# Cross attention on one core: ScalarE copies each V tile out of the shared PSUM bank, GpSimd splits the copy

## What is computed

```python
x = x + cross_attention(layernorm(x), ctx_1024, ctx_1024)   # x: 2 x 256 x 256, ctx: 2 x 4096 x 256
q = scale * (Q @ Wq + bq)        # 16 heads of 64
k = K @ Wk + bk
v = V @ Wv + bv
a = softmax(q k^T)
out = (a v) @ Wo + bo
```

## Time and profile before

| | us |
|---|---|
| median of 3 runs | 1417.87 |
| the three runs | 1412.96, 1418.12, 1417.87 |
| time of the profiled execution | 1414.05 |
| span of the profiled execution | 1412.1 |
| loop over the 128 steps, from about / to about | 43 / 1175 |

### The profile page before, as it was taken

One profiled execution on the slowest core, in us unless ns is written; L12 is line 12 of the kernel. 1 busy time (PEld: TensorE's weight loads), 2 busy tenths in 40 slices (PEclk: granted clock), 3 DMA queues, 4 the chain that ended last, 5 costly groups with the idle time before them and its releaser, 6 DMA issues. The chain is left out here.

```text
span 1412.1 us, 24618 instructions
## 1 busy us (share of the span) xinstructions
PE 1315.2 (93%) x9284; PEld 1121.4 (79%) x9284; DVE 1006.2 (71%) x1375; ACT 870.5 (62%) x1700; POOL 657.0 (47%) x797
## 2 busy tenths in 40 slices
PE   5899999999999999999999999999999996589857
PEld 5788888888888888888888888888888885267734
DVE  3666678667866777678767876787678767299666
ACT  3667666676667666676667666766676663256511
POOL 5655755475547553565457545754574440000000
PEclk9999999999999999999999999999999999699879
DMA  4010000000000000110000000000000000300000
GB/s 127 16 45 2 16 1 9 8 16 1 9 9 31 16 24 31 38 31 9 2 23 1 8 2 23 1 9 1 9 1 1 1 9 1 101 0 1 1 0 15
DMA packets 24901, 22.95 MB, mean 16 GB/s; under 512 B 4432, under 2 KB 24528, under 8 KB 24784
## 3 DMA queue, kind: packets, MB, share of 16 engines
q1 hardware_dynamic: 24784, 21.38, 5.0%
HBM read 20.85 MB, written 0.52 MB: 15 GB/s over the span
## 5 line engine op out<-in xcount | busy, mean ns | idle before, releaser
L548 ACT ACTIVATE pT_hi<-psT 128x512 fp32r<-128x512 f32 x512 | 292.4, 601 | 237.6 <-PE psT L320 222.5
L623 DVE TENSOR_TENSOR pT_lo<-psT,pT_hi 128x512 fp32r<-128x512 f32 x512 | 330.3, 684 | 105.4 <-ACT pT_hi L548 104.9
L617 DVE TENSOR_REDUCE negm<-psS 128x1 f32<-128x1024 f32 x256 | 311.7, 1218 | 51.2 <-PE psS L310 51.2
L267 POOL TENSOR_TENSOR kT<-kraw,khi 64x512 fp32r<-64x512 f32 x252 | 324.9, 1289 | 0.0
L513 ACT ACTIVATE prob<-psS,negm 128x1024 f32<-128x1024 f32 x256 | 285.7, 1116 | 1.0 <-DVE negm L617 1.0
L320 PE MATMUL psT<-ident,prob 128*128 128x128 f32 x2048 | 268.5, 274 | 3.9 <-DVE pT_lo L623 3.9
L261 POOL CAST khi<-kraw 128x512 fp32r<-128x512 f32 x126 | 76.9, 610 | 418.0 <-ACT kraw L523 416.6
L336 PE MATMUL psO<-pT_hi,v 128*128 128x256 f32 x1024 | 268.5, 294 | 1.2 <-DVE pT_lo L623 0.4
L320 PEld LDWEIGHTS psT<-ident,prob 128*128 128x128 f32 x2048 | 233.1, 140 | 38.8 <-issue 11.1
L337 PE MATMUL psO<-pT_lo,v 128*128 128x256 f32 x1024 | 256.7, 283 | 0.0
L336 PEld LDWEIGHTS psO<-pT_hi,v 128*128 128x128 f32 x1024 | 196.2, 192 | 2.7 <-DVE pT_lo L623 2.6
(11 more groups left out here) (215 smaller groups left out, 1563.9 us busy)
## 6 DMA issues: line engine op xcount, KB each, us to landing
cst<-in_ctx_dram SPq DMA_DIRECT2D x12, 512.0 KB, 3.8
oT<-in_ctx_dram SPq DMA_DIRECT2D x4, 512.0 KB, 5.3
wraw<-in_L_xattn_Wk_dram SPq DMA_DIRECT2D x8, 256.0 KB, 2.7
wraw<-in_L_xattn_Wv_dram SPq DMA_DIRECT2D x8, 256.0 KB, 2.7
wraw<-in_L_xattn_Wq_dram SPq DMA_DIRECT2D x8, 256.0 KB, 2.7
wo<-in_L_xattn_Wo_dram SPq DMA_DIRECT2D x8, 256.0 KB, 2.8
ff_wdn<-in_L_ffn_w_down_dram SPq DMA_DIRECT2D x1, 704.0 KB, 8.2
ff_win<-in_L_ffn_w_gate_dram SPq DMA_DIRECT2D x1, 640.0 KB, 5.3
```

Of the source, the lines that this page charges most:

```text
L267: pool.tensor_tensor(kT[half, m // 2 % KRING, h, 1, :], raw[own, :], khi[own, :].bitcast(F32), ALU.subtract).then_inc(k_split, 1)
L548: act.activation(pT_hi[:, i % PRING, :], psT[:, t % 2, :], ACT.Copy).then_inc(ph_ok, 1)
L617: dve.tensor_reduce(negm[:, g % 2, h, qt, c:c + 1], psS[:, qt, :], AX.X, ALU.max, negate=True)\
L623: dve.tensor_tensor(pT_lo[:, i % PRING, :], psT[:, t % 2, :], pT_hi[:, i % PRING, :].bitcast(F32), ALU.subtract).then_inc(pl_ok, 1)
```

## The change

A new SBUF tile `vraw` (128 x 512, fp32, one buffer) and a new semaphore `vraw_ok`. For m >= 4 ACT no longer writes the high part of V, but copies the bank to `vraw` (`v_copy`); it waits for `v_lo` to have reached m, that is for tile m - 1 to be split, before it overwrites `vraw`. POOL makes both parts from `vraw` in the new `split_v`, behind `split_piece` of the same step: a copy, then a subtraction. DVE's `v_low` is gone from the loop. TensorE's waits for the bank (`bank_free`, the one ahead of `turn_ctx`, the one behind the loop) are for `vraw_ok` in place of `v_lo`; `values` still waits for `v_lo`. The wait for the ring slot (`av_ok`) goes from ACT to POOL. The four tiles ahead of the loop are made as before.

```diff
@@ tiles and semaphores
+        vraw = tile("vraw", [P, 2 * GD])
...
-        v_ps, v_hi, v_lo = sem("v_ps"), sem("v_hi"), sem("v_lo")
+        v_ps, v_hi, v_lo, vraw_ok = sem("v_ps"), sem("v_hi"), sem("v_lo"), sem("vraw_ok")
@@ gpsimd
+            def split_v(m):
+                wait(pool, vraw_ok, m + 1 - FIRST)
+                if m >= VRING:
+                    old = m - VRING
+                    wait(pool, av_ok, 4 * (old // GH * GH + GH - 1) + old % GH + 1)
+                heads = vraw[:, :].rearrange("p (k h d) -> p k h d", k=2, h=GH)
+                pool.tensor_copy(v[:, m % VRING, :, :, 0, :], heads).then_inc(v_hi, 1)
+                wait(pool, v_hi, m + 1)
+                pool.tensor_tensor(v[:, m % VRING, :, :, 1, :], heads, v[:, m % VRING, :, :, 0, :].bitcast(F32),
+                                   ALU.subtract).then_inc(v_lo, 1)
+                wait(pool, v_lo, m + 1)
...
                 split_piece(n + LEAD)
+                split_v(n + LEAD)
@@ tensor, bank_free
                 else:
-                    wait(pe, v_lo, min(n + LEAD, N))
+                    wait(pe, vraw_ok, min(n + LEAD, N) - FIRST)
@@ tensor, end of a context step
                     wait(pe, cst_in, 16 * (u // KT - FIRST + 1))
-                    wait(pe, v_lo, n + LEAD + 1)
+                    wait(pe, vraw_ok, n + LEAD + 1 - FIRST)
                     turn_ctx(u, cst, psW[:, :])
@@ tensor, behind the loop
-                    pe.wait_ge(v_lo, N)
+                    pe.wait_ge(vraw_ok, N - FIRST)
@@ scalar
             def v_high(m, src):
                 wait(act, v_ps, m + 1)
-                if m >= VRING:
-                    old = m - VRING
-                    wait(act, av_ok, 4 * (old // GH * GH + GH - 1) + old % GH + 1)
...
+            def v_copy(m, src):
+                wait(act, v_ps, m + 1)
+                wait(act, v_lo, m)
+                act.activation(vraw[:, :], src, ACT.Copy).then_inc(vraw_ok, 1)
...
                 if n + LEAD < N:
-                    v_high(n + LEAD, psW[:, :])
+                    v_copy(n + LEAD, psW[:, :])
@@ vector
                 p_low(n, 3)
-                if n + LEAD < N:
-                    v_low(n + LEAD, psW[:, :])
```

## The result

The changed kernel takes 1404.13 us (median of 5 runs, 1402.24 to 1408.14). The kernel before, with two more runs than stood ahead of the prediction, has its median at 1413.68. The ratio is **0.9933, 95% interval 0.9917 to 0.9949**: 0.7% faster. The forecast was 1408.0 us and -0.70%. One execution of experiment 3 took 4681 us, 3.3 times the others, and stands in no median or ratio here.

The account below looks back on a forecast made before the run. TensorE, busy 93% of the span, was taken as the bound. Minus 9.9 us on the profiled 1414.05 gave 1404.2 (-0.70%); the same share off the median 1417.87 gave 1408.0 us, range 1401 to 1416.5.

Parts of the forecast that it names:

- rival B: Next step's first bank use waits for `prep_low` and takes the gain: 1418 or 1414 if all, 1413 if half; 26%.
- sign of being wrong: Among the listed signs: a turn of the bank that waits for `ctxT_lo` for 0.4 us.
- DVE's relief: In the loop, 124 removed subtractions take 86 us off DVE's row; gain 0 apart from the context turn's wait.
- The term: Context turn comes 0.12 us after the last matmul of `values`, not 0.55: 23 steps x 0.43 = 9.9 us gained.
- POOL's tight place: Steps 11 to 15 of groups 0 to 6, where POOL also splits weights and Q: covers of 0.2 to 0.7 us.
- Cost 0: POOL's added work in steps 11 to 15 of groups 0 to 6 was to cost TensorE nothing.
- stay near 10 us: Sign of being right: the waits of `k_raw` for POOL keep their total, 10.4 us in 7 waits before.
- Rival C's point: POOL late in steps 12 to 15 once its pair exceeds about 2.7 us; near 1458 at 4.1; 8%.
- the chain of covers: At a 2.7 us pair, four pairs' delays less about 1 us of cover: 1.4 us per group, 10 in all.
- The rule: VectorE and GpSimd share an SBUF port under an exclusive lock; expected not to bite in the loop, otherwise POOL is held.

Follow-up runs that it names:

- experiment 3: The changed kernel's path for V only in the 100 steps without a context turn, the old path in the 24 with it; 1417.82 us, 1.0006 of the kernel before.
- experiments 2 to 4: The first: the changed kernel's path for V only in the 24 context steps, 1404.49 us, 0.9934 of the kernel before; the others are experiment 3 and experiment 4.
- Experiment 8: The changed kernel with the split of the next V weights moved from GpSimd to VectorE in step 11; 1397.35 us, 0.9885 of the kernel before.
- experiment 5: The changed kernel with GpSimd writing the high part of V twice, one more copy per split; 1414.37 us, 1.0002 of the kernel before.
- Experiments 7 and 8: The first: the changed kernel plus a VectorE subtraction with two SBUF inputs in steps 10 to 15, 1405.68 us, ratio 0.9942; the second is Experiment 8.
- experiment 4: The changed kernel with an unused VectorE maximum over a constant tile in place of each removed subtraction; 1402.90 us, 0.9914 of the kernel before.
- experiment 10: The changed kernel with the context turn waiting for the split of V again, not for ScalarE's copy; 1537.55 us, 1.0866 of the kernel before.

## Why the prediction was right

*The mechanism and its size.* Point by point: the turn follows at 0.12 us in all 24 steps; the wait is gone, and in 22 of the 23 steps no other stands in its place (rival B falls). The wait for `ctxT_lo` that the prediction gave as a sign of being wrong is in the table, but it was there before, as long and as often. DVE's relief is worth nothing (experiments 2 to 4); the gain is that of the context steps alone. The term was 23 x 0.43 = 9.9 us, and the 23 steps gave 10.0. Two small errors cancel in it. Per step it is 0.45 to 0.46, because the scores also follow the turn 0.03 us closer (0.53 after its start, 0.56 before). And one gives nothing: the step from 11 to 12 of group 3. The prediction worked out POOL's tight place with the times of group 1 alone, where step 11 has no context turn; in group 3 the shorter step brings the next `k_raw` ahead of the end of POOL's split. Experiment 8 shows that this is the cause: with the split of the weights of V off POOL that step falls from 9.13 to 8.67 us.

That the profiled executions differ by just the 9.9 us of the term (1414.05 and 1404.13) is luck: beside the 10.0 us their spans gain 1.6 at the start and 0.4 in other steps, and lose 2.3 behind step 0 of group 7. For the share 0.70% was forecast and 0.67% measured.

*Rival B had a thin margin.* It gave ACT 0.08 us between `oT` and `prep_high`. The row shows 0.06 (61.64 against 61.20 + 0.38). It held because `oT` moves with `values`, as the prediction argued.

*POOL.* The pair takes 610 and 1281 ns, 2.05 us from start to free; strided writes cost POOL nothing. The piece of step 12 begins at 296.12, 1.3 us after `kraw` is written, and `k_raw` of step 14 waits 0.18 us, where 0.2 was forecast:

```profile
294.10 0.69 ACT L537 ACTIVATE kraw<-psW,bkT 128x512 f32<-128x512 f32 x1 [1.39 <-POOL kT L268]
...
311.02 0.69 ACT L537 ACTIVATE kraw<-psW,bkT 128x512 f32<-128x512 f32 x1 [0.18 <-POOL kT L268]
```

This wait comes once in each of six groups and stays under the cover of 0.44 us, so step 14 keeps its 8.22 us. The seventh new entry of the table is the wait of 0.42 us in step 12 of group 3, and TensorE does see it (0.20 us of waiting, 0.45 of step length not gained). "Cost 0" was wrong by this one step. The sentence that the waits "stay near 10 us" was right in the total (11.7) and missed that their number would double.

*Rival C's point.* "The pair takes over about 2.7 us": experiment 5 is that pair, and its ratio is 1.0002: the chain of covers gave 10 us of cost there, and 10 were measured. At 3.4 us the same way of counting gave 28 us over the changed kernel, and 34 were measured; among what it left out is the wait of `values` in step 0 of the next group.

*The rule.* The lock was rightly given little weight for this kernel, for the reason named: VectorE's large operations in the loop have at most one SBUF input, and GpSimd's 124 new subtractions take 1262 to 1305 ns. That the two engines can hold each other up, experiments 7 and 8 show; the last section has the numbers.

*What was mis-sized.* The absolute time was placed 3.9 us too high, since it was taken from a median of three runs, two of which lay near 1418. The profiled execution's own time gave 1404.2. With five runs the median of before is 1413.68. The share was the sounder number.

## What to carry to other kernels

When a kernel is bound by one engine, ask of each helper not how busy it is but which of its instructions that engine waits for; here 24 of 124 moved tiles carried the whole gain, through the moment at which a shared PSUM bank was handed on. A raw copy to SBUF frees a bank after one instruction, and the slow work may then run beside the rest, provided that the waits move with it: with the wait left on the slow work the changed kernel is 133 us slower. Before loading another engine, walk its queue through the fullest stretch and add up the covers, in each kind of step: a step that the change itself shortens has less cover. The average load (64%, 68%, 73% here) does not tell a free split from one that costs 34 us.

## What the runs showed of the hardware

VectorE and GpSimd do hold each other up when VectorE's operation has two SBUF inputs. Experiments 7 and 8 show it: GpSimd's copy of 512 numbers takes 0.95 to 0.96 us in place of 0.61, and VectorE's subtraction 1.50 and 1.65 in place of 0.68. The later of the two, be it that copy or that subtraction, ends 0.46 to 0.56 us after the first has ended. VectorE's copy from SBUF to SBUF, with one input, does it too: beside it GpSimd's two-input operation takes 1.45 us in place of 1.29 in six groups of experiment 8, and in group 3 GpSimd's copy 0.87 in place of 0.61. That copy takes VectorE 0.44 us for 512 numbers, where its subtraction takes 0.68. Operations with one SBUF input and the rest from PSUM, or a reduction of an SBUF tile, left GpSimd's times alone (experiment 4, and the kernels before and after). By the exclusive lock of the Trainium skill (SBUF — State Buffer, "SBUF: two separate sides"), which falls to VectorE operations with two SBUF inputs or in a 2-port mode, this is what should happen, and the traces agree; that VectorE's copy ran in such a mode no run here shows directly.

Behind the 24 pauses of 3.2 to 7.3 us of experiment 10 TensorE ran for a few microseconds at 1.2 GHz, and these slower stretches cost some 45 us on top of 88 us of waiting. In the loops of the kernels before and after, whose pauses are at most 1 us once step 0 is over, the granted clock was 1.00.
